# Second score products, exponentials and products with V one eighth of a unit nearer to the maxima

## The reference, cut to what matters

```python
q = einsum('oc,bct->bot', Wq, layernorm(x)) + bq      # k and v likewise, from the context
dot = einsum('bhdt,bhds->bhts', q, k) / 4
dot = mask * dot - (1.0 - mask) * 1e6
amap = softmax(dot, axis=-1) * mask
x = x + einsum('bhts,bhds->bhdt', amap, v)             # then x + experts(layernorm(x))
```

## Time and profile before

| | us |
|---|---|
| three runs, median (lowest to highest) | 652.69 (651.75 to 654.12) |
| the profiled execution, whole time | 654.27 |
| its span from first to last instruction | 652.4 |
| two passes alone, before unit 0 | about 37 to 61 |
| units 0 to 13, both passes side by side | about 61 to 430 |
| second passes of groups 30 and 31 alone | about 430 to 452 |
| expert block | 452 to 652 |

### The profile page before, as it was taken

How to read it: one execution, slowest core, us unless ns; L and a number is a source line. 1 busy time by engine, 2 the same in 40 slices (tenths; PEclk the granted TensorE clock), 3 DMA queues, 4 the chain that set the end, 5 groups by cost and what they waited for, 6 DMA issues and landing times.

```text
span 652.4 us, 12575 instructions
## 1 busy us (share of the span) xinstructions
PE 606.8 (93%) x4097; PEld 260.1 (40%) x4110; DVE 507.4 (78%) x970; ACT 472.3 (72%) x662; POOL 360.7 (55%) x494
## 2 busy tenths in 40 slices
PE   4799999999999999999999999888999999999987
PEld 3544332332332332333333332223554466666532
DVE  2478999999999999999999999964427744454577
ACT  3653899899899899899899888985442276667511
POOL 5458464575575575575575463341562577777410
PEclk9989999999999999999999999999999999999999
DMA  8641534534534535634433432115599533333178
GB/s 277 203 138 46 144 96 123 175 114 137 159 117 149 164 110 152 172 115 140 139 116 89 142 118 81 51 45 126 141 216 218 102 106 103 102 106 101 63 219 320
DMA packets 64990, 88.66 MB, mean 136 GB/s; under 512 B 12624, under 2 KB 45264, under 8 KB 63904
## 3 DMA queue, kind: packets, MB, share of 16 engines
q1 hardware_dynamic: 60032, 68.72, 34.6%
q0 software_dynamic: 4896, 19.14, 12.0%
HBM read 63.75 MB, written 32.74 MB: 148 GB/s over the span
## 4 chain that ended last, share of the span: by engine, by line
PE 76%; DVE 11%; issue 6%; ACT 5%; DMA 1%; POOL 1%; SPq 0%; ACTq 0%; DVEq 0%; POOLq 0%
PE PS L1083 17%; PE PS L986 11%; PE PS L1311 9%; PE PS L1055 8%; PE PS L1771 7%; DVE MX L996 7%; PE PS L845 5%; PE PS L1834 4%; PE PS L1585 4%; ACT E L1069 2%; PE PS L840 2%; PE PS L991 1%; PE PS L933 1%; PE PS L1732 1%; PE PS L929 1%
## 5 line engine op out<-in xcount | busy, mean ns | idle before, releaser
L996 DVE TENSOR_REDUCE MX<-PS 128x1 f32<-128x512 f32 x512 | 322.9, 683 | 17.4 <-PE PS L986 15.5
L1069 ACT ACTIVATE E<-PS 128x1024 f32<-128x1024 f32 x256 | 253.6, 1021 | 32.6 <-PE PS L1055 28.5
L986 PE MATMUL PS<-BIG 53*128 53x512 f16 x512 | 128.6, 384 | 12.1 <-DVE MX L996 10.6
L1083 PE MATMUL PS<-E,BIG 128*32 128x512 f32 x1024 | 136.4, 605 | 2.0 <-ACT E L1069 2.0
L1055 PE MATMUL PS<-BIG 55*128 55x512 f16 x512 | 101.3, 381 | 8.2 <-ACT E L1069 3.5
L879 POOL TENSOR_TENSOR ML<-BIG,ML 128x512 f32<-128x512 f32 x30 | 38.3, 1278 | 101.2 <-ACT BIG L855 101.0
L986 PEld LDWEIGHTS PS<-BIG 53*128 53x128 f16 x512 | 34.3, 93 | 133.9 <-DVE MX L996 119.6
L1793 DVE SCALAR_TENSOR_TENSOR E<-WP,PS 128x352 bf16<-128x352 f32 x39 | 20.3, 521 | 45.5 <-ACT WP L1783 45.5
L855 ACT ACTIVATE BIG<-PS,BIG 128x256 f32<-128x256 f32 x64 | 35.8, 561 | 27.5 <-PE PS L840 16.1
L1771 PE MATMUL PS<-BIG,CT 128*128 x312 | 52.9, 313 | 1.0 <-DVE WP L1346 1.0
L1853 POOL DMA_INDIRECT scr_ys<-SW,bvB x39 | 38.4, 984 | 19.1 <-DVE SW L1846 10.2
(11 more groups left out here) (261 smaller groups left out, 915.6 us busy)
## 6 DMA issues: line engine op xcount, KB each, us to landing
scr_parts<-WP SPq DMA_DIRECT2D x96, 128.0 KB
BIG<-scr_parts SPq DMA_DIRECT2D x64, 192.0 KB
BIG<-in_we POOLq DMA_DIRECT2D x8, 1088.0 KB, 13.8
scr_u<-ML SPq DMA_DIRECT2D x32, 256.0 KB, 3.0
X<-in_x SPq DMA_DIRECT2D x8, 512.0 KB, 6.7
CT<-in_ctx SPq DMA_DIRECT2D x8, 512.0 KB, 4.5
ML<-scr_u SPq DMA_DIRECT2D x16, 256.0 KB
ML<-scr_recs SPq DMA_DIRECT2D x16, 256.0 KB
```

The costliest lines, as they stand in the source:

```text
L986: e.matmul(PS[:, yi[name] % 3, :], QK[rows, qb(u), 0, j0 + jj, 128 * tt:128 * tt + 128], QK[rows, qb(u), 1, j0 + jj, :], start=True, stop= ...
L996: e.tensor_reduce(MX[:, g % 2, c:c + 1], PS[:, yi[name] % 3, :], AX.X, ALU.max)\
L1069: e.activation(E[:, st, 2 * jj:2 * jj + 2, :], PS[:, slot(name):slot(name) + 2, :], ACT.Exp, scale=1 / 1024).then_inc(s["rc"], 1)
L1083: ins = e.matmul(PS[32 * hh:32 * hh + 32, AVB, :], VT[:, b % 2, st, 4 * (g % 4) + hh, :], E[:, st, hh, :], start=(st == 0), stop=(st == 3))
```

## The change

All of the second pass moves one eighth of a unit ahead (`AHEAD = 1`), with what follows it: X, exponentials, AV, the copying out, the store, and the whole of `finish_unit` but for its last reciprocal, which stays at 16.99. The offsets inside a step are turned by one place, so that the positions at which PE meets an X or an AV stay what they were and only another step stands there: where step st of group g stood, step st+1 stands, and step 0 of the next group stands where step 3 stood. The first pass, the projections and the experts' block keep their positions.

N moves on its own, from 1.25 and 5.25 to 0.6 and 4.6. The ring of one unit becomes: X 0.15, X 0.5, N 0.6, X 0.9, X 1.1, X 2.1, X 2.15, X 2.75, X 3.65, Q 3.75, X 4.15, X 4.5, N 4.6, Q 4.75, X 4.9, X 5.1, X 6.1, X 6.15, K 6.65, X 6.75, X 7.65, K 7.85. ACT's copy of AVB moves from 4.4 to 3.4 and from 8.4 to 7.4, each time from behind the exponential of the X pair at 4.15 (8.15) to ahead of the exponential of the X pair at 3.65 (7.65). The reciprocals of DVE move from 5.22, behind the maxima of S 5.1, to 4.22, between the maxima of S 4.05 and of S 4.4. On SP the placing of the maxima moves from 1.55 and 5.55 to 0.9 and 4.9; the spreading of the reciprocals, which stood behind it at 5.88, stands just ahead of it at 4.88; the store of AVB moves from 5.2 and 1.2 to 4.2 and 0.2.

The small products behind the last four S products of group 1 are left out: the first AV now comes sooner after them.

```diff
--- before.py
+++ after.py
@@ -32,6 +32,7 @@
 KP = (0, 0, 1)
 NK = 55
 IT = 1 / 8
+AHEAD = 1
 WHOLE = 2
 WARM = (3, 1)
 SPLIT = ((-0.08, 0.19), (0.01, 0.39), (0.05, 0.43), (0.24, 0.31), (0.35, 0.4))
@@ -258,10 +259,10 @@
         for g in range(NG):
             for st in range(4):
                 for jj in range(2):
-                    ring.append((g / 2 + (st + ((0.15, -0.1, 0.1, -0.25), (0.5, 0.1, 0.15, 0.65))[jj][st]) * IT, ("x", g, st, jj)))
+                    ring.append((g / 2 + (st - AHEAD + ((0.15, -0.1, 0.1, -0.25), (0.5, 0.1, 0.15, 0.65))[jj][st - AHEAD]) * IT, ("x", g, st, jj)))
                     for a in range(2):
                         mring.append((g / 2 - 1 + (st + ((0.05, -0.2, 0.1, -0.05), (0.4, 0.1, 0.3, 0.45))[jj][st] + .01 * a) * IT, ("s", g, st, jj, a)))
-            ring.append((g / 2 - 1 + 5.25 * IT, ("n", g)))
+            ring.append((g / 2 - 1 + 4.6 * IT, ("n", g)))
         for w in range(NU):
             ring += [(w - 3 + 3.75 * IT, ("q", w, 0)), (w - 3 + 4.75 * IT, ("q", w, 1)),
                      (w - 3 + 6.65 * IT, ("k", w, 0)), (w - 3 + 7.85 * IT, ("k", w, 1))]
@@ -987,7 +988,7 @@
                                      QK[rows, qb(u), 1, j0 + jj, :], start=True, stop=True).then_inc(s["mp"], 1)
                             if g == 0 and tt == jj == a == 0:
                                 e.wait_ge(s["id"], 6)
-                            for _ in range(WARM[g] if g < 2 else 0):
+                            for _ in range(WARM[g] if 4 * g + tt < 7 else 0):
                                 e.matmul(PS[:, AVB, 0:256], identb[:, :], ident[:, :].bitcast(BF), start=True, stop=True)
 
                         def mx(e, tt=tt, jj=jj, a=a, name=name):
@@ -1041,7 +1042,7 @@
 
         def attend(g):
             u, j0, b = g // 2, 2 * (g % 2), g // 4
-            t0 = g / 2
+            t0 = g / 2 - AHEAD * IT
             for st in range(4):
                 for jj in range(2):
                     name = ("x", g, st, jj)
@@ -1084,7 +1085,7 @@
                                        VT[:, b % 2, st, 4 * (g % 4) + hh, :], E[:, st, hh, :],
                                        start=(st == 0), stop=(st == 3))
                     ins.then_inc(s["av"], 1)
-                pe.at(t0 + (st + (1.62 if g >= 30 else (1.25, 1.3, 1.05, 1.2)[st])) * IT, av)
+                pe.at(t0 + (st + (1.62 if g >= 30 else (1.25, 1.3, 1.05, 1.2)[st - AHEAD])) * IT, av)
 
             def evac(e):
                 e.wait_ge(s["av"], 4 * g + 4)
@@ -1100,7 +1101,7 @@
 
         def finish_unit(u):
             b, o = u // 2, u % 2
-            t0 = u + 1 + 6 / 32
+            t0 = u + 1 + 6 / 32 - AHEAD * IT
 
             def read(e):
                 e.wait_ge(s_u[0], 16 * (u + 1))
```

## The result

The changed kernel takes 664.7 us (median of 4 runs, 662.0 to 665.8), the kernel before 652.2 beside it: ratio 1.0172, 95% interval 1.0152 to 1.0192. It is slower, as forecast, by 12.5 us in the medians and by 9.8 us in the two profiled executions (664.11 against 654.27). The forecast was 661.1.

What follows compares the result with a forecast made beforehand. PE, DVE and ACT are nearly full at once mid-attention; the first pass sets the pace, PE only just ahead. 10.4 + 0.6 - 2.6 = +8.4 us on 654.27 gives 662.7, or 661.1 from the median; range 650.0 to 667.5.

Steps and rivals of the forecast that it cites:

- The slot behind N: In units 0 to 12, Q behind N waits for the exponential of X 4.5; 0.25 to 0.70 us a unit.
- the recovery: In each unit, DVE's two other waits, 0.25 and 0.20 us, can swallow up to 0.45 us of its lateness.
- The small terms: ACT's copy of AVB ahead of an exponential, 0.2 us a unit, and N at 0.6 holding X 1.1, 0.1 us.
- Units 13 and 14: The units without Q get the small terms alone: a loss of 0.3 us each, 0.6 us in all.
- The end: After the last maxima, seven second-pass steps remain instead of eight; a gain of 2.6 us, bounded below by 2.04, carried in full.
- The placing: From N to its group's first X, 6.6 us remain where 4.5 are needed; in time, nothing counted.
- its rival: Landing over 3 us behind the issue makes step 0's X wait in 32 groups; about 676 us, chance 0.06.
- The stall swallowed: PE's 0.9 us fit into PE's and DVE's own waits, only the end counts; 650.1 us, chance 0.16.
- the cancelling: Loss in the units and gain at the end cancel, 0.05 to 0.35 us a unit; 652 to 655 us, chance 0.12.
- The clock: PE's clock falls around 60 us for want of the small products; 656 us if the rest cancels, chance 0.02.
- The rule on regimes: Interleaving regimes, a second-pass step moved from the end into the start, would cut the time by the drained step.
- the start: Ahead of unit 0, where DVE sets the pace, the four small products left out are worth nothing.

Runs made afterwards that it cites:

- run 1: The kernel before with only N moved early, to 4.6 and 0.6 instead of 5.25 and 1.25; 666.6 us, ratio 1.0215.
- run 9: The changed kernel with N of second halves at 4.85 (4.6 in the last two units) and ACT's copy of AVB at 4.65; ratio 1.0059, 690.9 us on a slower chip.
- run 2: The changed kernel with N of the second half at 4.85, behind Q, instead of 4.6; 659.8 us, ratio 1.0127.
- run 10: The changed kernel with ACT's copy of AVB at 4.65 instead of 4.4; 701.0 beside 687.4 us on another chip, ratio 1.0224.
- run 6: The changed kernel with the first early load of expert weights moved behind unit 14's additions; 665.7 us, ratio 1.0185.
- run 8: The kernel before with the first early load of expert weights moved behind unit 14's additions; 657.3 us, ratio 1.0068.
- run 5: The changed kernel with N at 5.15 and 1.15 instead of 4.6 and 0.6; 662.2 us, ratio 1.0179.
- run 11: The kernel before with the second pass an eighth early from group 28 on alone, N of those groups at 4.6 or 0.6; 652.4 beside 653.8 us, ratio 0.9976.
- run 4: The changed kernel with ACT's copy of AVB at 4.75 instead of 4.4; 673.6 us, ratio 1.0324.

## Why the prediction was right, and where its sum was off

- **The slot behind N** (forecast: Q starts 1.19 us later, PE idle 0.9, 0.25 to 0.70 us a unit left, 0.5 taken). The mechanism is shown from both sides: N alone brings more than the whole loss (13.9 against 11.8 us in units 0 to 12), N behind Q takes 8.1 of the 11.8 away. Q started 0.06 us behind the exponential (forecast 0.07), PE stood 0.81 us, DVE 0.94. The size is 0.65 to 0.70 us a unit in the steady part, near the upper end, and 8.1 / 13 = 0.63 on average. The step that was mis-sized is the recovery: DVE's short waits of a unit were to swallow up to 0.45 us, and half of it was taken. But the two that were counted, 0.25 and 0.20 us, lie in first halves, behind the next division, and the 0.23 of the same half lies ahead of the stall; almost none lies behind it. N alone lengthens the second halves by 1.09 and 1.19 us, nearly all of the 1.19, except in units 1, 3 and 5, where 0.50 us of waits did lie behind it. What is given back in the changed kernel is the reciprocals' place, 0.47 of the forecast 0.49 us: in group 17 DVE is 1.09 us late at the S pair 4.8 and 0.62 behind the place where the reciprocals stood. The miss of this term is 8.1 - 6.5 = 1.6 us.
- **The small terms** (0.2 for ACT's copy, 0.1 for N at 0.6). Their sum, what is left with N at 4.85, is 0.38 against 0.3 in the steady part, and 3.7 against 3.9 us over units 0 to 12. N at 0.6, read from the first halves of run 1, costs 0.27 - 0.09 = 0.18 us in two units, 0.09 a unit, as forecast. The copy's share is what a later copy gave back in the first halves (run 9 against run 2): 0.17 + 0.07 = 0.24 in two units, 0.12 a unit (run 10 against the changed kernel: 0.15 in two units, 0.08), below the forecast 0.2. The other 0.17 us or more of the 0.38 were not taken apart. That the copy would wait 0.95 us for AV once a unit was not in the working. Its remedy was judged wrongly: later copies cost more than they brought.
- **Units 0 to 12**: 11.8 us measured, 10.4 forecast, bounds 3.3 to 15.6; a unit of the steady part takes 25.4 us (forecast 25.2). **Units 13 and 14**: -0.25 instead of +0.6; without a Q the small terms don't show either.
- **The end** (2.6 us forecast, 2.0 to 2.6): 2.9 up to the experts, a little above the upper bound. "I carry the gain in full" was the step that failed: 1.4 us come back at the experts' last wait. The prediction let the store, the read and the reciprocals move with the last AV, but the spreading of unit 14 had moved beside a load that did not move, because POOL's order ties it to the last maxima (it went out 11.0 us behind the last division in both kernels, the spreading 16.3 us behind it before and 11.6 after).
- **The placing** was in time with N at 4.6, as worked out, and its rival would have been the case with N left where it was: there it fell short by up to 3.5 us. **The stall swallowed** and **the cancelling** needed at most 0.35 us a unit; it was 0.91 on average. **The clock** was 1.00 from 60 to 440 us, and 0.73 in the one stretch from 30 to 40 us where it was 0.69.
- **The rule on regimes.** The Trainium skill (Perfetto Trace Analysis, Optimization Strategy) says that interleaving a kernel's regimes may improve performance. The end did get shorter by a step, and the last groups alone are 0.2% ahead of the kernel before; done in all groups it costs four times what it brings (11.8 against 2.9 us). The price lies where three engines are full.
- Net: +9.8 us in the profiled executions against +8.4. Two terms came out worse (the slot by 1.6 us, the end by 1.2) and three better (units 13 and 14 by 0.9, the start by 0.3, the small terms by 0.2), so the total is nearer than its terms were; that much is luck. The medians differ by 12.5, because the profiled execution of before lay 2.1 us above its median and that of after 0.6 below.

## What to carry to other kernels

Before moving one item in a ring of slots, write down for each of its neighbours whose reader it now waits for; an item that slips between a producer and the one two places behind it costs that one a whole run of the reader (here 1.02 us of exponential), and an in-order engine hands this on to everything behind. Where full engines meet, only waits that lie behind the stall, before the next point that sets the pace, can swallow it (0.5 us in units 1, 3 and 5, almost nothing in the others); if none is seen there, take the upper bound. If only the end profits from a closer distance, close it in the last groups, behind the place that would pay for it.

## What the runs showed of the hardware

- **A small DMA behind a large load lands with it.** 16 KB take 1.5 us (median of the page); with the load out of the way the same spreading took 1.8 us in run 6 and 2.7 in run 8. Behind the load of 1,088 KB from another queue it lands when the load has landed: issued 0.6 us after it in the changed kernel, at 461.8 us (the load at 461.6); 1.4 us after it in run 5, at 459.7 (459.2); 2.0 us after it in run 8, at 462.0 (461.8); 5.3 us after it in the kernel before, at 451.6 (450.1). In the 11 traces that show both landings the distances of issue are 0.6 to 5.6 us, and the small one always lands 0.2 to 1.8 us behind the load, never ahead of it. From the load in the changed kernel:

```profile
BIG<-in_we POOLq DMA_DIRECT2D x1, 1088.0 KB, 9.2
...
scr_recs<-RC SPq DMA_DIRECT2D x1, 16.0 KB, 8.7
```

  (KB of one, median us from issue to landing.) The Trainium skill (DMA: Bandwidth & Descriptors, Queues, rings and completion order) says that each DMA engine takes turns between its queues, a packet at a time. Taken alone that would let 16 KB land long before 1,088 KB; none of the 11 traces shows that, and what holds the small one these runs don't tell.
- **Executions of one kernel differ by their granted clock.** The kernel before, 22 times beside run 11: 651.5 to 654.3 us at a mean of 0.995 or more, 654.7 and 655.3 at 0.992, 657.0 to 657.7 at 0.987 to 0.989, and 656.9 and 657.4 at 0.984. In the traces such a fall is one stretch: in run 11 the mean is 0.56 from 630 to 640 us, near the lower of the clock's two levels (0.5 of full speed), and the products there come 4.5 us later than in the kernel before. A median of four can be off by some us for it. Whether an order of work makes such falls more frequent (the four of run 4 all had 0.990, those of run 1 all 0.995 or more) no run was made to tell.
- **The start differs between executions of the same code.** The kernel before and the one with only a later expert load are identical up to there, and their divisions of group 0 lie 3.1 us apart in time since the span's start, while the intervals behind agree within 0.03 us. For a few tenths of a per cent the intervals of the steady part told more than the spans.
- **One chip was slower in the experts alone.** In run 9 (and in run 10, 234.9 us) the attention took what it does elsewhere, and the stretch from the experts to the end 233.4 instead of 200.4 us, at a mean granted clock of 0.94 (columns as in the earlier trace rows); the page shows a slice at 0.6 there.

```profile
453.20:686.60 233.40, 203.73 (x1262) 112.61 (x1258) 112.15 (x202) 94.45 (x160) 105.24 (x108) 0.94 0.46 128
...
PEclk9899999999999999999999999999999699989999
```

PE was busy for 204 us of these 233 where it was busy for 192 of 200, so at most about 12 of the 33 us go by the clock; what the rest is, no run of this study was made to tell.
